# Attention over 16 heads: score tiles three groups ahead on VectorE, one exponential over three tiles, 32-column identity tiles

## The reference

```
h = layernorm(x);  k, v, q = split(h @ w_in, 3)        # 16 heads of 8 columns
scores = q @ k^T / sqrt(8) + bias[head, key - query]   # per batch and head 1024 x 1024
attn   = softmax(scores) @ v
x = x + a * sigmoid(g)          with a, g = split(attn @ w_gate + b_gate)
x = x + ffn_fp8(layernorm(x))   # one product with values rounded to fp8
```

## Time and profile before

| | us |
|---|---|
| median of 3 runs | 640.92 |
| the runs | 640.6, 643.98, 640.92 |
| the profiled execution, its own time | 643.61 |
| span of the profiled execution, first to last instruction | 641.8 |

### The profile page before, as it was taken

The page is one execution under the profiler, slowest core; times in us unless marked ns, Lnnn a source line. Parts: engine busy times, 40 slices in busy tenths (PEclk is TensorE's granted clock), DMA queues, the critical chain, the costliest instruction groups (busy, mean ns, idle before and its releaser), DMA issues.

```text
span 641.8 us, 12665 instructions
## 1 busy us (share of the span) xinstructions
PE 585.9 (91%) x3989; PEld 158.5 (25%) x3989; DVE 567.8 (88%) x692; ACT 549.5 (86%) x600; POOL 105.6 (16%) x95
## 2 busy tenths in 40 slices
PE   5893499999999999999999999999999999989775
PEld 2451022222222222222222222222212221234432
DVE  5974499999999999999999999999999998935976
ACT  2763499999999999999999999999999999933453
POOL 5731600010101010110101010101010101105603
PEclk8797599999999999999999999999999999989855
DMA  9126551616161525344352516161616163300004
GB/s 233 50 65 177 150 118 29 143 25 139 29 132 42 127 51 110 71 90 93 70 117 50 119 42 135 27 135 27 138 27 138 29 133 81 75 11 1 1 1 131
DMA packets 29803, 53.88 MB, mean 84 GB/s; under 512 B 9317, under 2 KB 20970, under 8 KB 28650
## 3 DMA queue, kind: packets, MB, share of 16 engines
q1 hardware_dynamic: 29466, 53.35, 36.6%
q10 hardware_dynamic: 320, 0.33, 0.2%
HBM read 43.34 MB, written 9.16 MB: 82 GB/s over the span
## 4 chain that ended last, share of the span: by engine, by line
ACT 29%; issue 26%; DMA 10%; SPq 8%; PE 6%; DVE 5%; POOL 4%; ACTq 1%; POOLq 0%
ACT pbuf L985 12%; ACT split L985 12%; DMA r_scratch<-dc 5%; DMA qb<-m_scratch 4%; PE ps L1163 2%; SPq L236 2%; SPq L242 2%; ACT pbuf L993 2%; ACT split L993 2%; DVE kb L1397 1%; DMA rd<-r_scratch 1%; POOL kb L845 1%; SPq L258 1%; PE ps L908 1%; PE ps L1165 1%
## 5 line engine op out<-in xcount | busy, mean ns | idle before, releaser
L942 DVE TENSOR_TENSOR pbuf<-ps,t 128x1024 f32<-128x1024 f32 x192 | 229.9, 1217 | 22.6 <-PE ps L883 18.6
L942 DVE TENSOR_TENSOR split<-ps,t 128x1024 f32<-128x1024 f32 x192 | 231.7, 1223 | 12.0 <-PE ps L883 6.6
L985 ACT ACTIVATE pbuf<-pbuf 128x1024 f32<-128x1024 f32 x192 | 202.8, 1196 | 21.3 <-DVE pbuf L942 20.9
L883 PE MATMUL ps<-qb,kb 64*128 64x512 f16 x1024 | 183.7, 390 | 24.2 <-SPq L798 14.7
L985 ACT ACTIVATE split<-split 128x1024 f32<-128x1024 f32 x192 | 198.3, 1203 | 0.6 <-DVE split L942 0.6
L908 PE MATMUL ps<-split,vst 128*32 128x512 f32 x1024 | 136.0, 604 | 1.0 <-ACT split L993 1.0
L908 PE MATMUL ps<-pbuf,vst 128*32 128x512 f32 x1024 | 136.6, 606 | 0.0
L883 PEld LDWEIGHTS ps<-qb,kb 64*128 64x128 f16 x1024 | 47.8, 93 | 309.2 <-DVE pbuf L942 113.9
L892 PE MATMUL ps<-t64s,ident 128*64 128x512 f16 x512 | 80.5, 395 | 0.0
L993 ACT ACTIVATE split<-ps 128x1024 f32<-128x1024 f32 x64 | 74.5, 1164 | 0.0
L993 ACT ACTIVATE pbuf<-ps 128x1024 f32<-128x1024 f32 x64 | 74.0, 1156 | 0.0
(11 more groups left out here) (140 smaller groups left out, 351.9 us busy)
## 6 DMA issues: line engine op xcount, KB each, us to landing
t<-g_scratch SPq DMA_DIRECT2D x16, 960.0 KB
kb<-k_scratch SPq DMA_DIRECT2D x120, 64.0 KB
t64s<-gh_scratch SPq DMA_DIRECT2D x16, 248.0 KB
t64s<-gl_scratch SPq DMA_DIRECT2D x16, 248.0 KB
qb<-q_scratch SPq DMA_DIRECT2D x60, 64.0 KB
x_sb<-in_L_attn_x SPq DMA_DIRECT2D x4, 512.0 KB, 6.5
q_scratch<-split SPq DMA_DIRECT2D x8, 256.0 KB, 3.3
k_scratch<-split SPq DMA_DIRECT2D x8, 256.0 KB, 3.6
```

Source lines behind the costliest of these rows:

```text
L883: last = eng.matmul(ps[:, u + c, :], kb[p][rows, keys], qb[p][rows, b * HALF:(b + 1) * HALF], start=True, stop=True)
L942: eng.tensor_tensor(slot(g, b), banks(unit(k), 2), t128[p][:, t * P:t * P + S], ALU.add).then_inc(z_ready, 1)
L985: eng.activation(buf, buf, ACT.Exp).then_inc(p_ready, 1)
```

## The change: what it does

- VectorE's three tiles of a group are issued three groups ahead (`LEAD` = 3), the fourth tile stays two ahead (`LAG` = 2). TensorE's order within a group becomes products c = 0, scores 0 and 1, products c = 1, scores 2 and 3.
- ScalarE takes the fourth tile first and then one exponential over the group's three slots (3072 columns). The fourth tile has a semaphore of its own (`pd_ready`).
- The identity matmul of the fourth tile is eight matmuls of 32 columns in place of four of 64; the bias parts are loaded 32 columns wider.
- The copies of VectorE stand at group `LEAD` - 1, the reciprocal at group 6.

```diff
-RECIPROCAL = 3
+LEAD = 3
+RECIPROCAL = 6
...
-T64W = 2 * S - 64
+T64W = 2 * S - 32
...
+        def slots(g, n):
+
+            k = 4 * (g % SETS)
+            return big[:, k * S:(k + n) * S] if k < 8 else splitf[:, (k - 8) * S:(k - 8 + n) * S]
...
                         if g:
-                            eng.wait_ge(p_ready, i * (8 * GPH) + 4 * g)
+                            eng.wait_ge(pd_ready, i * (2 * GPH) + g)
...
-                        for m in range(2):
-                            c0 = t * P + 64 * m + c * HALF
-                            last = eng.matmul(ps[64 * m:64 * m + 64, u + c, :], ident2[:, :],
+                        for m in range(4):
+                            c0 = t * P + 32 * m + c * HALF
+                            last = eng.matmul(ps[32 * m:32 * m + 32, u + c, :], ident2[:, 0:32],
...
                     if c == 0:
-                        eng.wait_ge(p_ready, i * (8 * GPH) + 4 * (g + 1))
+                        eng.wait_ge(pd_ready, i * (2 * GPH) + (g + 1))
+                        eng.wait_ge(p_ready, i * (2 * GPH) + (g + 1))
...
+                for g in range(LEAD):
+                    for b in range(B if g < LAG else DPG):
                         scores(0, g, b)
...
+                        products(i, g, 0)
+                        ahead(i, g + LEAD, (0, 1))
+                        products(i, g, 1)
+                        ahead(i, g + LEAD, (2,))
+                        ahead(i, g + LAG, (3,))
...
-                            if b == 0 and g == LAG - 1:
+                            if b == 0 and g == LEAD - 1:
...
+                        eng.wait_ge(sp_ready, i * (2 * GPH) + (g + 1))
+                        eng.wait_ge(groups_done, i * (2 * GPH) + (g + 1))
+                        eng.activation(slot(g, DPG), banks(4, 2), ACT.Exp).then_inc(pd_ready, 1)
+                        if g == LAG - 1:
+
+                            with eng.If(i > 0):
+                                eng.wait_ge(groups_done, i * (2 * GPH) + SETS)
+                                eng.wait_ge(o_stored[1], i * (16 * B))
+                                copy_half(eng, 1, 1).then_inc(o_ready[1], 1)
...
+                        eng.wait_ge(z_ready, i * (2 * DPH) + DPG * (g + 1))
+                        eng.activation(slots(g, DPG), slots(g, DPG), ACT.Exp).then_inc(p_ready, 1)
```

More of the change, by code:

```diff
@@ L725, in attention_block @@
         p_ready = sem("p_ready")
+        pd_ready = sem("pd_ready")
         num_in = [sem(f"num_in{b}") for b in range(B)]
@@ L914, in products, with ahead @@
                         last.then_inc(half_done, 1)
-                for g in range(LAG):
-                    for b in range(B):
+                def ahead(i, g, tiles_of_group):
+                    if g < 2 * GPH:
+                        for b in tiles_of_group:
+                            scores(i, g, b)
+                    else:
+                        with eng.If(i < NH2 - 1):
+                            for b in tiles_of_group:
+                                scores(i, g, b)
+                for g in range(LEAD):
+                    for b in range(B if g < LAG else DPG):
                         scores(0, g, b)
@@ L958, in _ @@
                                     copy_half(eng, 1, 0).then_inc(o_ready[0], 1)
-                            if b == 0 and g == GPH + LAG - 1:
+                            if b == 0 and g == GPH + LEAD - 1:
                                 eng.wait_ge(half_done, i * 2 + 1)
@@ L980, in _ @@
                     for g in range(2 * GPH):
[L981 to L1003, removed]
@@ new lines, in _ @@
+                        if g == SETS // 2:
+                            eng.wait_ge(qk_out, 16 * 4 * B)
+                        eng.wait_ge(sp_ready, i * (2 * GPH) + (g + 1))
[6 more added lines that the diff above has]
+                                copy_half(eng, 1, 1).then_inc(o_ready[1], 1)
@@ L1004, in _ @@
+                        if g == GPH + LAG - 1:
+                            eng.wait_ge(groups_done, i * (2 * GPH) + (GPH + SETS))
+                            eng.wait_ge(o_stored[0], i * (16 * B) + 16 * B)
+                            copy_half(eng, 0, 1).then_inc(o_ready[1], 1)
+                        eng.wait_ge(z_ready, i * (2 * DPH) + DPG * (g + 1))
+                        eng.activation(slots(g, DPG), slots(g, DPG), ACT.Exp).then_inc(p_ready, 1)
                 eng.wait_ge(groups_done, H * GPH + SETS)
```

## The result

The changed kernel takes 694.08 us (median of 4 runs, 691.79 to 702.39) against 641.97 for the kernel before: the ratio is 1.0796, with a 95% interval of 1.0764 to 1.0828. Ratios, here and in the experiments, leave out runs in a second, slower state of the chip, such as that of 702.39 us. The kernel is slower, as forecast, but by more than the forecast of 679 us says, and the time lies just above the range, which ended at 692. The profiled execution took 691.79 us, that of before 643.61: 48.2 us more.

What follows compares the result with a forecast made beforehand. Waits between engines were to make a group 3.86 us and late loads a half 32.9, against 30.48: fourteen halves +33.7, first +4.3, last -0.8, sum +37 on 640.9, 678, with some lateness 679 us; range 655 to 692.

Steps and rivals of the forecast that it cites:

- the wait for the load: TensorE at the next head's first scores: 1.45 us of wait in each half, in place of 1.95 to spare.
- the ring through the big exponential: TensorE to ScalarE and back, fourth tile's exponential first: 3.87 us a group, 3.86 taken.
- hidden loads: Rival: loads stay hidden, only the waits between engines cost; half 31.36 us, +14 us, 655 us; chance 0.12.
- loads alone: Rival: only the loads cost, the group stays at 3.75 us or less; half 32.55, 673 us; chance 0.08.
- the faster one: Rival: the change does what its parts promise, ScalarE and TensorE both at 3.56 us a group; 616 us; chance 0.05.
- ScalarE's relief: One exponential over three tiles: ScalarE's work falls from 3.75 to 3.56 us a group, useful only if ScalarE bounds.
- The sum without late loads: Whole kernel: median before, 640.9, plus 37 us, its loads taken as ordinary: 678 us.
- The sum against the profiled execution: Whole kernel: 643.6 plus 37, plus 7.8 for four late loads losing their spare 1.95 us each: 688 us.
- The length behind S0: From the next head's first scores to the next half's load issue: 10.6 plus 1.8 us.
- The ring through ScalarE: Identity matmuls, fourth tile's exponential, big one, products, back to identity matmuls: 4.41 plus 3.34, 7.75 us for two groups.
- The ring of the add: TensorE to VectorE: tile 2's scores wait 0.26 us for tile 0's add to free banks; group 3.56 + 0.26 = 3.82.
- I to P: TensorE, start of the fourth tile's identity matmuls to start of the next products half: 0.48 us taken, from 0.48 to 0.56.

Runs made afterwards that it cites:

- e1: Changed kernel with the bias loads made for the first two heads only, later heads reusing them: 664.62 us, 1.0368 of the kernel before.
- e9: Changed kernel with bias loads for two heads only and ScalarE's order turned (big exponential, copy, fourth tile): 641.35 us, ratio 0.9993.
- e4: Changed kernel with full loads, product halves again between the scores of tiles 0, 1 and 2: 725.83 us, 1.1309 of the kernel before.
- e8: Changed kernel with bias loads for two heads only and product halves again between the scores of tiles 0, 1 and 2: 641.26 us, ratio 0.9982.
- e10: Changed kernel with bias loads for two heads only and three one-tile exponentials in place of the big one: 675.55 us, ratio 1.0544.
- e3: Changed kernel with LEAD = 2 in place of 3: 672.05 us, 1.0481 of the kernel before.

## Why the prediction was right and wrong

**The direction and both mechanisms** held: the wait for the load, in all 14 halves, and the ring through the big exponential behind the fourth tile's. In shares of the kernel before's time the loss is 0.0796: e1 takes 0.0428 of it away (load), e9 a further 0.0375 (ScalarE's order), and nothing is left. The shares hold in this order alone: with full loads, e4 has a shorter group and is slower. The rivals of hidden loads and of loads alone are both out, as is the faster one. ScalarE's relief (3.56 a group) could not have been had with TensorE's order: in e9 the big exponential is no longer in the ring, and the time is that of before, since TensorE's order with the wait for the add takes 3.75.

**The step that failed: "So the ordinary load is usable at 312.5 + 0.8 = 313.3, 20.45 after the 292.86".** It was read from one half of the kernel before, where nothing waits for the load, and was put at 20.5 by S0's start. In the changed kernel, where S0 does wait in each half, issue to S0 is 21.18 on average over 14 halves (19.98 to 23.26; the half shown above has 20.60). That is 0.68 us a half, 9.5 us. The sum without late loads was 678 and the profiled execution took 691.8; of these 14 us the rest is the first issue (5.9 later and not 4.3: 1.6), the clock in one half (1.2, below) and terms of under 1 us each. Why one load takes 20 us and the next 23 is open. I had also taken the late loads of the profiled execution for an accident that the median would be free of; the median of 694 shows that they are not. The sum against the profiled execution, 688, came within 4 us of its 691.8, in part by luck: it added 7.8 us for four late loads, and what was measured is lateness in nearly all of them. The 679 was that sum with the late loads taken out.

**Smaller terms.** The length behind S0, 12.4, was right to 0.1, so the reciprocal at group 6, costed at nothing, shows no cost there; no run has it alone. The last half was put at -0.8 where its own numbers (8 x 3.86 + 0.48 - 1.8 against 30.48 - 0.3) give -0.6; measured, nothing is left for it. The group was 3.91, not 3.86, and not even: 3.74 and 4.08 in turn. The ring through ScalarE was 7.82 for two groups, not 7.75: the release of the products took 0.14 (328.55 - 328.41), where I had 0.06 from a scores' wait; these products wait for two semaphores. The ring of the add was 3.75, not 3.82: I to P is 324.50 - 324.06 = 0.44 and P to S behind it 325.46 - 324.50 = 0.96, where I took 0.48 and 1.00. The ring through ScalarE was summed with the wait for the add in it (the 1.81 of 1.00 + 1.81 + 0.53 = 3.34; measured 3.33), and e8 bears out that it matters there. The big exponential was 2.76, as against 2.78. The eight identity matmuls took 0.61, as four did: they do run four abreast.

The Trainium skill's rule that a change of tiling mode drains TensorE (TensorEngine Tiling (Array Packing), Key Properties) fits: from 32-column identity matmuls it is 0.44 to the 32-column products, and 287.47 - 286.92 = 0.55 to the scores, which have other tiles (e8). The Trainium skill's warning on PSUM evacuation (the same page, Performance Considerations, PSUM Bottleneck) points at the wait of S2 for the add, which is real (S0 to S2 1.80 in e9). But it came with the order of the scores and not with faster tiles: the identity matmuls took 0.61 in place of 0.62.

**What the sum left out:** the clock. In one half of the changed kernel (TensorE idle for 3.85 us for a load) the clock fell, as in e4:

```profile
240.00:242.00 2.00, 2.00 (x20) 0.63 (x20) 1.91 (x2) 0.00 (x0) 0.23 (x1) 0.50 0.04 8
```

```profile
237.91 0.61 PE L890 MATMUL ps<-qb,kb 64*128 64x512 f16 x4 [3.85 <-DMA qb<-m_scratch]
238.44 1.66 PE L917 MATMUL ps<-pbuf,vst 128*32 128x512 f32 x8
```

From these scores to the next issue it is 13.61 us, where the other halves have 12.45: a load that is late enough costs more than its lateness, here by 1.2 us.

## What to carry to other kernels

Before more work is issued ahead, look at what the first item of it waits for: here one group of lead moved the next head's first scores onto its load, and a shorter group was worth nothing while TensorE waited for that load (e4). Moving a short instruction that triggers a transfer (the copy, 0.6 us, one place earlier) was worth 22 us; joining three exponentials into one was worth 11 (e10 against e1). And where two engines hand tiles round, add up the ring, each wait with its release time: joining three exponentials saves 0.2 us of ScalarE, but put behind the late tile, and with a wait for an add elsewhere in the same turn, they lengthen two groups from 7.50 to 7.82.

## What the runs showed of the hardware

- Products that wait for two semaphores started 0.14 us (0.15 in e3) after the later one's instruction ended; scores that wait for one, 0.06.
- Behind 32-column identity matmuls, 32-column products started after 0.44 us, scores after 0.55 (e8). Scores followed the products behind identity matmuls after 0.96, those behind other scores after 1.00.
- Eight identity matmuls of 32 columns took 0.61 us, as four of 64 columns did (0.62).
- In the changed kernel the granted clock was 0.50 behind TensorE's wait of 3.85 us, and stayed at 1.00 through the 13 other waits for a load, of 0.57 to 2.69 us. In e4 it was 0.50 around all 14 waits, of 2.67 to 5.50 us. So the length of the wait alone does not tell: of two waits of nearly the same length, the changed kernel's left the clock at 1.00 and e4's did not. Their rows, the changed kernel's first:

```profile
373.43 0.61 PE L890 MATMUL ps<-qb,kb 64*128 64x512 f16 x4 [2.69 <-DMA qb<-m_scratch]
```

```profile
373.00:375.00 2.00, 1.57 (x12) 0.36 (x12) 1.06 (x1) 0.28 (x1) 0.00 (x0) 1.00 0.14 33
```

```profile
532.87 0.61 PE L890 MATMUL ps<-qb,kb 64*128 64x512 f16 x2 [2.67 <-DMA qb<-m_scratch]
```

```profile
533.00:535.00 2.00, 2.00 (x10) 0.20 (x8) 1.23 (x1) 0.92 (x1) 0.00 (x0) 0.50 0.25 59
```
